# Attention output kept with its channels on the partitions and normalised at load, and maxima turned by an element-wise DMA

## The reference

```python
x = x + 0.5 * ffn(layernorm(x))      # base matmul + 8 rank-16 experts, top 2 per token
x = x + attn(layernorm(x))
x = x + 0.5 * ffn(layernorm(x))

# attn: 32 query heads, 8 key/value heads of 16 channels, signed (+1/-1) weights with a scale per output channel
q, k, v = bitnet_linear(h, ...)      # x @ sign(w).T * (mean|w| * scale), then nan_to_num(+-1e6)
scores = einsum('bhqd,bhkd->bhqk', q, k) / 4
attn = softmax(scores); out = einsum('bhqk,bhkd->bhqd', attn, v)
return bitnet_linear(out, o_weight, o_scale)
```

## Time and profile before

| | |
|---|---|
| median of 3 runs | 1158.16 us (1157.06 to 1159.91) |
| profiled execution | 1159.3 us, span 1157.5 us |
| PE busy | 93% |
| DVE busy | 73% |
| ACT busy | 63% |
| POOL busy | 25% |
| granted TensorE clock, mean | 0.967 |

### The profile page before, as it was taken

How to read it: one execution, slowest core, us unless ns; L and a number is a source line. 1 busy time by engine, 2 the same in 40 slices (tenths; PEclk the granted TensorE clock), 3 DMA queues, 4 the chain that set the end, 5 groups by cost and what they waited for, 6 DMA issues and landing times.

```text
span 1157.5 us, 16340 instructions
## 1 busy us (share of the span) xinstructions
PE 1076.3 (93%) x5968; PEld 484.5 (42%) x5968; DVE 844.4 (73%) x1146; ACT 727.1 (63%) x1361; POOL 293.3 (25%) x485
## 2 busy tenths in 40 slices
PE   5989887999999999999999999999999999998857
PEld 3778661344334433344334333433343334333436
DVE  5766679767776778877888678777977887782173
ACT  6457432757865787675776567666766675768420
POOL 5365556302510250410140014003200320041010
PEclk9989886999999999999999999999999999999979
DMA  7122331021210113011210121031002001300300
GB/s 254 38 90 88 101 103 49 28 65 26 61 34 32 30 53 83 27 32 38 68 27 26 53 54 26 26 81 27 26 26 80 27 27 26 81 6 7 90 1 36
DMA packets 87359, 59.42 MB, mean 51 GB/s; under 512 B 44144, under 2 KB 73328, under 8 KB 87280
## 3 DMA queue, kind: packets, MB, share of 16 engines
q1 hardware_dynamic: 87280, 58.39, 17.6%
HBM read 37.64 MB, written 20.32 MB: 50 GB/s over the span
## 4 chain that ended last, share of the span: by engine, by line
PE 74%; DVE 12%; ACT 6%; POOL 3%; issue 3%; DMA 1%; SPq 1%; DVEq 0%; POOLq 0%
PE ps_out L1452 20%; PE ps_score L1440 18%; PE ps_max L1415 16%; PE ps_fill L1373 5%; DVE neg_max L1218 3%; ACT probs L954 3%; PE ps_fill L1400 2%; PE ps_fill L1341 1%; PE ps_fill L1355 1%; PE ps_fill L1377 1%; DVE neg_max L1043 1%; DVE zd L1110 1%; PE ps_out L1373 1%; PE ps_max L1429 1%; PE ps_fill L1347 1%
## 5 line engine op out<-in xcount | busy, mean ns | idle before, releaser
L954 ACT ACTIVATE probs<-ps_score 128x512 f32<-128x512 f32 x992 | 539.0, 597 | 272.5 <-PE ps_score L1440 270.8
L1218 DVE TENSOR_REDUCE neg_max<-ps_max 128x1 f32<-128x1024 f32 x480 | 572.1, 1220 | 168.6 <-PE ps_max L1415 167.0
L1415 PE MATMUL ps_max<-kst,qst 96*128 96x512 bf16 x1024 | 294.0, 388 | 14.6 <-DVE neg_max L1043 5.7
L1440 PE MATMUL ps_score<-qst,kst 99*128 99x512 bf16 x992 | 305.1, 385 | 1.2 <-ACT probs L954 0.8
L1452 PE MATMUL ps_out<-probs,v_ring 128*32 128x512 f32 x2048 | 273.6, 606 | 8.1 <-ACT o_sb L960 5.3
L1440 PEld LDWEIGHTS ps_score<-qst,kst 99*128 99x128 bf16 x992 | 77.8, 97 | 254.3 <-ACT probs L954 210.0
L1415 PEld LDWEIGHTS ps_max<-kst,qst 96*128 96x128 bf16 x1024 | 88.4, 98 | 143.3 <-issue 17.6
L793 POOL CAST shift<-neg_max 128x16 bf16<-128x16 f32 x32 | 7.5, 236 | 463.3 <-DVE neg_max L1218 458.9
L1452 PEld LDWEIGHTS ps_out<-probs,v_ring 128*32 128x32 f32 x2048 | 41.0, 108 | 101.9 <-issue 92.0
L889 ACT ACTIVATE xn<-xc,ln_shift,rstd 128x512 f32<-128x512 f32 x48 | 38.5, 811 | 30.0 <-POOL ln_shift L690 19.0
L1373 PE MATMUL ps_fill<-wb_h,xt_h 128*128 128x512 f32 x84 | 46.9, 559 | 1.6 <-DVE xc L1205 0.8
(11 more groups left out here) (254 smaller groups left out, 1331.8 us busy)
## 6 DMA issues: line engine op xcount, KB each, us to landing
qst<-q_dram SPq DMA_DIRECT2D x192, 64.0 KB, 2.2
q_dram<-zm SPq DMA_DIRECT2D x24, 256.0 KB, 2.6
kst<-k_dram SPq DMA_DIRECT2D x192, 32.0 KB, 2.2
xc<-x SPq DMA_DIRECT2D x8, 512.0 KB, 3.8
x_dram<-xc SPq DMA_DIRECT2D x8, 512.0 KB, 2.8
xc<-x_dram SPq DMA_DIRECT2D x8, 512.0 KB, 4.2
out<-xc SPq DMA_DIRECT2D x8, 512.0 KB, 3.2
att_dram<-att SPq DMA_DIRECT2D x31, 128.0 KB, 2.2
```

Source lines behind the costliest of these rows:

```text
L954: act.activation(probs[:, kt % 2, j, :], score_bank(i, uu, j), ACT.Exp, scale=1.0 / HD ** 0.5).then_inc(probs_ready, 1)
L1218: dve.tensor_reduce(neg_max[:, uu % 2, t:t + 1], ps_max[max_slot(uu, pos)][:, :, :], AXY, ALU.max, negate=True).then_inc(max_read, 1)
L1415: last = pe.matmul(ps_max[slot][:, half, :], qst[0:SR, r, j, q * P:(q + 1) * P], kst[0:SR, r, half * 512:half * 512 + 512], start=True, st ...
L1440: pe.matmul(score_bank(i, uu, j), kst[0:SR + PARTS, uu, kt * P:(kt + 1) * P], qst[0:SR + PARTS, uu, j, :], start=True, stop=True).then_inc ...
```

## The change

The maxima stay in float32. SP stores `neg_max` (128 x 16) element by element into DRAM as 16 x 128 (`store_max`), loads it back as 16 rows (`load_max`), GpSimd splits the 16 x 128 rows into the three parts (`split_shift`, now in slot 5 and for the very next unit), and SP writes them into `qst` as before. The turn on TensorE is gone, with `copy_rows`.

`o_sb` is stored as it is, channels and sums. The back loads 32 x 8 rows of sums as 128 x 64 (`sums`), inverts them (`NR`), stores them, loads them again, each repeated over 16 partitions, into `zd` (`NL`), and multiplies the output with them on VectorE (`N0a`, `N0b`); ScalarE and VectorE then make `xt_h` and `xt_l` from SBUF. `xn` and `zd` of the two slots alternate between chunks. In the tail, the last unit's output and sums go by 8 DMAs per chunk from `o_sb` into place (`load_last_out`). One empty entry of `BACK` is taken out later on, so that the steps from `Oa` to `R5` come half a slot later.

```diff
 BACK =
-    12 * [""] + ["T0a", "T0al", "", "T0b", "T0bl", "", "Oa0", "Oa1", "C0", "Ob0", "Ob1", "", "G0 C1", ...
+    8 * [""] + ["NR", "NL", "", "", "", "", "", "N0a", "N0al N0b", "N0bl", "", "Oa0", "Oa1", "C0", "Ob0", "Ob1", "", "G0 C1", ...
-    "R0", "R1", "R2 HT0", "R3 R4 HT1", "R5", "", "", "WR", ...
+    "R0", "R1", "R2 HT0", "R3 R4 HT1", "R5", "", "WR", ...
 # SP
+            def store_recip(ch):
+                sp.wait_ge(recip_ready[ch.att], ch.att_use + 1)
+                sp.dma_start(recip_dram[a, 0:known, :].rearrange("h (g t) -> h g t", g=groups),
+                             sums[ch.att][0:known * groups, :]).then_inc(recip_stored[ch.att], 16)
+            def load_recip(ch):
+                sp.wait_ge(recip_stored[ch.att], (ch.att_use + 1) * 16)
+                for c in range(DC):
+                    sp.dma_start(recip_t[ch.att][0:(h1 - h0) * HD, c, :],
+                                 recip_dram[a, h0:h1, :].unsqueeze(1).broadcast_to([h1 - h0, HD, CH])
+                                 ).then_inc(recip_loaded[ch.att], 16)
+            def load_last_out(ch):
+                sp.wait_ge(o_copied, NU)
+                for j in range(REP):
+                    for dst, r0 in ((att_t[ch.att], 32 * j), (recip_t[ch.att], 32 * j + HD)):
+                        sp.dma_start(dst[to, DC - 1, :], o_sb[r0:r0 + HD, (NU - 1) % 2, s * CH:s * CH + CH]
+                                     ).then_inc(last_out_loaded[s], 16)
+            def store_max(i, uu):
+                sp.wait_ge(max_read, max_done(i, uu))
+                sp.dma_start(max_dram[uu % 2, :, :].rearrange("t p -> p t"), neg_max[:, uu % 2, :],
+                             allow_slow_non_contiguous=True).then_inc(max_stored[uu % 2], 16)
+            def load_max(i, uu):
+                sp.wait_ge(max_stored[uu % 2], 16 * (n + 1))
+                sp.dma_start(max_rows[:, uu % 2, :], max_dram[uu % 2, :, :]).then_inc(max_rows_loaded[uu % 2], 16)
             def body(i, plan, load_next, first=False, last=False):
-                    if kt == 2 and not (last and uu == 3):
-                        load_rows(i, uu + 1, turn_use(i, uu, last))
-                    if kt == 4 and not (first and uu == 0):
-                        store_att(i, uu - 1, turn_use(i, uu, last))
-                    if slot == 5 and load_next is not None:
+                    if kt == 0 and not (last and uu == 3):
+                        store_max(i, uu + 1)
+                    if kt == 3 and not (last and uu == 3):
+                        load_max(i, uu + 1)
+                    if kt == 6 and not (last and uu == 3):
+                        load_rows(i, uu + 1)
+                    if kt == 1 and not (first and uu == 0):
+                        store_att(i, uu - 1)
+                    if slot == 2 and load_next is not None:
+                        load_att(load_next)
+                    if slot == 4 and load_next is not None:
                         load_x1(load_next, chunk_loaded[0])
-                        load_att(load_next)
 # GpSimd
-                    if kt == 7 and not (last and uu >= 2):
-                        split_shift(i, uu + 2)
+                    if kt == 5 and not (last and uu == 3):
+                        split_shift(i, uu + 1)
 # ScalarE
+                if pos in ("N0a", "N0b"):
+                    act.wait_ge(att_normed[s], n * 2 + (t + 1))
+                    act.activation(xt_h[s][:, :, t * P:(t + 1) * P], att_t[ch.att][:, :, t * P:(t + 1) * P],
+                                   ACT.Copy).then_inc(xt_h_ready[s], 1)
 # VectorE
+                if pos in ("N0a", "N0b"):
+                    dve.wait_ge(att_loaded[ch.att], (ch.att_use + 1) * 16 * DC)
+                    dve.wait_ge(recip_loaded[ch.att], (ch.att_use + 1) * 16 * DC)
+                    dve.tensor_tensor(att_t[ch.att][:, :, tok], att_t[ch.att][:, :, tok], recip_t[ch.att][:, :, tok],
+                                      ALU.mult).then_inc(att_normed[s], 1)
-                    if kt == 1:
-                            copy_rows(i, uu + 1, use, at, max_read if first and uu == 0 else rows_copied)
-                            normalise(i, uu - 1, use, at)
 # TensorE
-                    if kt == 1:
-                        turn(i, uu, turn_use(i, uu, last), turn_slot(uu, last), rows=not (last and uu == 3),
-                             out=not (first and uu == 0))
```

More of the change, by code:

```diff
@@ L62 @@
 TAIL_LAG = 7
-START_TURN = 11
-START_USES = 33
+START_USES = 32
 FRONT_ON_DVE = ("clamp", "sum")
@@ L156, in __init__ @@
         self.sum0 = n * 3 if self.front else 3 * FRONT_PAIRS + n * 2
-        self.load = (n + 1) * 16 if self.front else 16 * FRONT_PAIRS + n * 48 + (32 if tail else 48)
+        self.load = (n + 1) * 16 if self.front else 16 * (FRONT_PAIRS + n + 1)
+        self.att = slot if tail else n % 2
+        self.att_use = (n // 2 if slot == 0 else 3) if not self.front else 0
         self.mb0 = n * NF if self.front else NF * FRONT_PAIRS + n * NB
@@ L578, in body @@
                         load_x1(tail[1], x1_loaded[1])
+                    if last and slot == 8 * UB - 3:
+                        for ch in tail:
+                            store_recip(ch)
+                    if last and slot == 8 * UB - 2:
+                        for ch in tail:
+                            load_recip(ch)
                     for half in (2 * slot - 2, 2 * slot - 1):
@@ L628, in _ @@
             body(7, back_plan(ch), ch, last=True)
+            for ch in tail:
+                load_last_out(ch)
             load_x1(tail[0], x1_loaded[0])
@@ L1211, in fill @@
                                       ALU.mult).then_inc(filler_read[bnk], 1)
-            def reduce_pair(i, uu, pos, t):
-                use = max_use(i, uu, pos)
-                dve.wait_ge(max_scores, use + 1)
-                if t == 0 and (not isinstance(i, int) or UB * i + uu >= 0):
-                    dve.wait_ge(shift_parts, i * (4 * UB) + 4 * (uu + 1))
-                dve.tensor_reduce(neg_max[:, uu % 2, t:t + 1], ps_max[max_slot(uu, pos)][:, :, :], AXY, ALU.max,
-                                  negate=True).then_inc(max_read, 1)
@@ L1256, in body @@
                         fill(item)
-                    if kt == 1:
-                        use, at = turn_use(i, uu, last), turn_slot(uu, last)
-                        if not (last and uu == 3):
-                            copy_rows(i, uu + 1, use, at, max_read if first and uu == 0 else rows_copied)
-                        if not (first and uu == 0):
-                            normalise(i, uu - 1, use, at)
-                    for pos, t in pairs[:1]:
-                        reduce_pair(i, uu, pos, t)
+                    if last and slot == 8 * UB - 4:
+                        for ch in (Chunk("back", 0, 6, tail=True), Chunk("back", 1, 0, tail=True)):
+                            invert_sums(ch)
+                    for t in pairs[:1]:
+                        reduce_pair(i, uu, t)
                     for item in plan.get(2 * slot, []):
                         fill(item)
-                    for pos, t in pairs[1:]:
-                        reduce_pair(i, uu, pos, t)
+                    for t in pairs[1:]:
+                        reduce_pair(i, uu, t)
             for ch, step in ALONE_DVE:
@@ L1513, in _ @@
             times_v(8, -1, KT - 1)
-            turn(8, 0, max_use(7, 2, 2), max_slot(2, 2), rows=False)
             for item in tail_steps():
```

268 lines of the change are left out of this document (136 added, 132 removed).

## The result

The changed kernel takes 1213.6 us (median of 4 runs, 1210.8 to 1216.2) against 1158.9 us for the kernel before in the same job. The ratio is 1.0474, 95% interval 1.0455 to 1.0494: 4.7% slower. The forecast was 1146.5 us, the range 1136 to 1167; the time is outside both. In the profiled executions the span grows from 1157.5 to 1210.0 us.

What follows compares the result with a forecast made beforehand. PE, busy 93% of the span, was taken as the bound. Terms -28.2 - 0.3 + 10.8 + 3.0 + 1.0 + 2.0 = -11.7 us on the profiled 1159.3; the median is 1.1 lower: forecast 1146.5 us, range 1136 to 1167.

Steps and rivals of the forecast that it cites:

- the rows' way through SyncE: Chain of stores and loads before the next unit's scores; element-wise store 4.9 us, PE waits 0.5 us per unit 0: +3.0.
- the wall: Upper bound of 6.8 us on the element-wise store's time, from a load of 128 single floats; beyond it, Rival C.
- The rule of the Trainium skill: Strided last dimension: one descriptor per element; rearranged plain DMA 19 times slower than hardware transpose; would put the store far over 4.9 us.
- Rival C: Element-wise store takes 10 us or more; in unit 0 DVE, then PE, stop: 27 us more, 1173 us; chance 0.18.
- the jam: Slot 0 of unit 1, bodies 2 to 7: three new DVE operations and ACT's copies delay PE 1.8 us each, +10.8.
- The rows' wait itself: Start of unit 1, six bodies: PE waits 0.5 us each for the row writes, between 0 and 2.5: +3.0.
- The turn and T0: Work removed from PE: 31 turns in the loop at 0.75 us, -23.3; T0, 0.82 us in six bodies, -4.9.
- The tail: From the end of the loop to the first projection matmul: transfers, inversion and product add +2.0 us, between 0 and 5.
- The rows' wait in the front: In the front, rows come late behind `S1` on POOL, once per body: +1.0 us in all.

Runs made afterwards that it cites:

- e3_actq: The changed kernel with the element-wise store of the maxima issued from ACT's DMA queue instead of SyncE's: 1207.5 us, ratio 1.0419.
- e10_act: e9_best with ACT's `xt_h` copies of the two products half a slot later in ACT's order: 1150.2 us, ratio 0.9929.
- e5_vturn: The changed kernel, but DVE turns the 32x32 blocks of `neg_max`, so the maxima leave in 128 runs of 128 bytes: 1168.6 us, ratio 1.0082.
- e4_out: The output half of the change alone; the maxima still turned on PE and copied out by DVE as before: 1163.7 us, ratio 1.0025.
- e8_late: e5_vturn with stores before loads, rows before inverses, normalisation spread over slots 8 to 11, `x1` loaded after the inverses: 1163.0 us, ratio 1.0039.
- f1_line: The changed kernel, its 2048 single floats stored 8 bytes apart, each partition's in its own 128 bytes; rows from `x`, exponentials' scale 1e-6: 1221.3 us.
- e9_best: e8_late with the tail's sixteen small transfers issued half by SyncE, half by ACT, and the last inversion in two halves: 1160.4 us, ratio 1.0018.

## Why the prediction was wrong

**The step that failed** is the element-wise store in "the rows' way through SyncE". I took 4.9 us from loads of 256-byte pieces; from its issue to what it frees it takes about 11 (10.7 in the rows above). I even had the wall in the text ("beyond it is a rival below") but gave it 0.18. The row I was nearest to was a load of long pieces; what I priced was a write of 4-byte pieces. The one row with 4-byte pieces, 128 of them in 6.8 us, was a load as well, so no row had the direction, and 6.8 was no upper bound. The rule of the Trainium skill ("DMA: Bandwidth & Descriptors", "Rules for kernel authors") that I set against the change pointed the right way, though its factor of 19 is against another operation; that each element goes by itself agrees with the 2064 packets of a store in e3_actq. Against a store of runs the factor here is 11 / 1.8, about 6.

**Rival C had the mechanism and half the price.** The output's store behind, DVE stopping in slot 4, PE within a slot, all as written. It gave 27 us; 50.4 + 6.4 = 56.8 us over the forecast for the unit 0s were measured. It counted one wait per body, and that wait was nearly right: the stops are 33 us. Against the 140.0 us that the unit 0s take in e10_act, the changed kernel's 199.2 are 59.2 more: 33 of stops, 7.8 of waits for the rows, and 18 that I did not split, of the lower clock behind the stops (about 2 us each) and the jam at the border.

**The rows' wait itself** was too small in the sum: +3.0, 0.5 in each body. It is 7.8 us in the changed kernel, and still 7.7 in e5_vturn, whose store lands long before the 4.9 us I had given it. Between the 12 loads and the rows stand 14 DMAs, not 13, and the store of the inverses, 2.2 us in my sum, took 4.4 us in body 2 of e5_vturn, where PE's wait for the rows is longest (3.95 us), and 4.4 in body 4 of the changed kernel.

**The turn and T0** were right once nothing hid them. The front's units got 0.71 us shorter each (forecast 0.75). In units 2 and 3 it is 0.5 per turn, its lower bound. In unit 0, e10_act has 23.34 us: 1.46 less than 24.80, where 0.75 + 0.82 = 1.57 was forecast. In e4_out (bodies 4 to 6) and e8_late, both at 24.8, the jam had eaten it.

**The jam**: size near, cause half right. Forecast 1.8 us per body, all in unit 1. In e4_out PE waits 0.88 us in bodies 4 to 6, which falls into unit 0. In bodies 2 and 3 it waits 3.0 and 2.9, because there the inverses come late too (DVE waits 2.0 us for `zd`). Behind the wait the granted clock was 0.50 in body 3 and 0.64 in body 7, with unit 1s of 29.8 and 29.6 us where bodies 4 to 6 have 27.9. I named ACT's second copy as the culprit; e8_late shows that the first suffices, with 1.10 us. The clock was not in my sum at all.

**The tail**: +6.6 instead of +2, outside its bounds of 0 to 5. From the last copy to the first projection it takes 10.95 us against 6.24. DVE shows the two mis-sized terms:
```profile
1143.20 1.75 DVE L1249 RECIPROCAL zd<-zd 64x256 f32<-64x256 f32 x1 [7.28 <-DMA zd<-o_sb]
1144.98 0.69 DVE L1251 TENSOR_TENSOR xn<-xn,zd 128x512 f32<-128x512 f32 x1
```
I took the inversion of 256 columns as 0.5 us, and it takes 1.75; the eight issues come every 0.63 us, not every 0.45. Together 2.7 us. The rest, 1.9 us, lies behind the first projection. A second inversion of 1.75 us stands there on DVE, at 1152.18, which the sum doesn't have; that it is the cause is not shown.

**The rows' wait in the front**, +1.0 in my sum, did not show: those units are shorter by nearly the turn's whole price (5.0 of 5.25 us).

## What to carry to other kernels

Before a transfer is put on a path, ask for its piece size and direction, and treat a price from another size as no price: a cheap turn on an engine that leaves runs (0.21 us on DVE) beat a free-looking one in the access pattern. Price a stop of PE with its followers: what else is queued behind the waiting instruction, and the granted clock afterwards. In an in-order engine, an instruction waiting for late data belongs behind the work that is due, even if half a slot later.

## What the runs showed of the hardware

- Store to DRAM, issue to landing: 2048 pieces of 4 bytes 10.7 (unit 1 above) to 11.6 us (f1_line), 1024 of 4 bytes as long as 2048 (SyncE's longest wait is 10.5 for both), 128 of 4 bytes 7.8, 1024 of 8 bytes 5.5, 128 of 64 bytes 1.8; 2048 pieces of 4 bytes read, 3.6.
- Meanwhile a 256 KB store on another queue lands in 10.5 us instead of 2.1.
- In e8_late the same PE gap of 1.10 + 0.19 us is followed by a lower granted clock (0.50 in the next 3 us of body 5) in two of six bodies, at +1.65 us, and not in the other four. Behind the six stops of 3.7 to 9.2 us in the changed kernel it was 0.50 to 0.67 each time.
- RECIPROCAL on DVE takes 1.75 us for 64x256 f32, 0.95 for 64x128 (e9_best) and 0.55 for 128x64.
